# Two score banks of every third block move from ScalarE to VectorE as a bit-and-polynomial exponential

## The chip, the cores and the metric

The program runs on all 8 cores of one Trainium2 chip, each with its own 2048 tokens and no traffic between the cores. The metric is the device time in microseconds of the slowest core. Engines are named as in the profile: PE is TensorE, PEld its weight loads, DVE VectorE, ACT ScalarE, POOL GpSimd, SP SyncE. A matmul result lies in PSUM, which has 8 banks of 512 fp32 values in each of 128 partitions.

## The reference, cut to what matters

```python
x = x + attn(layernorm(x))           # first half
x = x + moe(layernorm(x))            # second half: top-1 router, 8 experts, relu
# attn, for each token and its 16 heads of 64 features:
Q = (X @ W_q + b_q) * scale; K = (X @ W_k + b_k) * scale; V = X @ W_v + b_v
Q, K, V = (t.reshape(n, heads, l, d) for t in (Q, K, V))
scores = jnp.einsum('neax,nebx->neab', Q, K)
A = jax.nn.softmax(scores, axis=2)
diag = jnp.diagonal(A, axis1=2, axis2=3)
out = (diag[..., None] * V).reshape(n, l, hid) @ W_o + b_o
```

The softmax runs along one axis and then only the diagonal is kept. So of every column of the score matrix only two numbers are needed: the exponential of its diagonal entry and the sum of the exponentials of all its entries. Because of the plain reshape, all 8192 entries of a column come from 512 neighbouring tokens and their 16 feature groups, so that a core works on four independent windows of 512 tokens.

## The kernel before, in words

**Windows, tiles, blocks.** NR = 4 windows w of 512 tokens, each of four tiles t of 128 tokens. A block r (0 to 63 in a window) is one tile with one feature group gb of its keys (r = 16 t + gb) against the 16 groups of queries: 16 matmuls of 64 rows by 512 columns, one PSUM bank each (line 443). A tile is 16 blocks.

**Slots.** ACT takes the exponential of 3 or 4 banks with one instruction, which also sums along the row (lines 563 and 567; the sum leaves ACT as a second instruction, ACTIVATION_READ_ACCUMULATOR). Such a group is a slot n. `SLOTS` gives the sizes of a block's five slots, (3,3,4,3,3) and (3,3,3,4,3) by turns; even slots use banks 0 to 3 and odd slots banks 4 to 6. PE may write slot n when ACT has done slot n-2 (`aE`), and ACT may read slot n when PE has written it (`pSCR`). A slot's sum is one column of ZC. The first `PLAIN` blocks of a window (18, 2, 2, 2) take the diagonal entry off before the exponential (line 563, as bias); the others need not when a bound on the scores, found on the chip for each window, is at most `LIMIT` (line 567).

**The fill.** All other work of PE goes through one bank, number 7 (`ONE_BANK`). It is a chain of generators, `fill`: the projections of the next window (query, key, value: 8 matmuls of 512 columns each), swaps and diagonals of the keys, and for each finished tile `tail`: the diagonal weights, the output projection, the residual, the router. After the matmuls of each slot PE takes units from this chain, by credits: a slot of 3 gives 1.5, a slot of 4 gives 2.5 (`SPARE`), a matmul of 512 columns costs 1. A yielded 0 ends the turn, and so does a yielded None (`breath`, at each job's start) if the turn has already done something. `hold` keeps the tail of tile t from beginning before block 16(t+1)+1 in the same window. At a window's end what is left of the chain is run without slots in between. PE calls `bank()` before each job and waits there for `vM`, until DVE has emptied bank 7 of the job before; everything PE does is in one order, so the next slot stands behind that wait.

**DVE** reads bank 7 job by job, in the same order (`bank()`, `query`, `key`, `value`, `swap_k`, `tail`). `PIECES` lists which jobs go into which tail. The key jobs are in the last two tiles of a window, for the window that follows. In `tail` DVE waits for the tile's last exponential (`aE`), sums ZC and goes on (lines 756 to 762, and on to 812, the last instruction of a tile's tail).

**Around it.** At the same time POOL issues the casting copies of the expert weights (w1b, w2b), one after the other. When the four windows are done the experts run. They are bound by PE; the change does not touch them.

Of the kernel before, what the change touches and what calls it, by code (L numbers as in the profile page):

```python
# [43 lines left out]

SLOTS = ((3, 3, 4, 3, 3), (3, 3, 3, 4, 3))
SPB = 5
SPH = 64 * SPB
SPT = 16 * SPB


# [16 lines left out]
LIMIT = 60.0  # L67
PLAIN = (18, 2, 2, 2)
ALL_BANKS = (7, 6, 5, 4, 3, 2, 1, 0)
# [3 lines left out]
def build_nc():  # L73
# [26 lines left out]
    with ExitStack() as st:  # L100
# [13 lines left out]
        XN2 = S("XN2", [P, 4, 1024], BF16)  # L114
# [44 lines left out]
        ZERO = S("ZERO", [P, 512], BF16)  # L159
# [48 lines left out]

        def piece_done(u):

            eg, i = divmod(u, NPC)
            return NCK * eg + (8 * i + 8 if i < 4 else NF + 2 * (i - 4) + 2)
# [14 lines left out]
        def _(e):  # L227
            ring, base, kM = ALL_BANKS, 0, 0

            def bank():  # L230
# [4 lines left out]
                kM += 1  # L235
                return ring[(kM - 1 - base) % len(ring)]

# [10 lines left out]
            def breath():  # L248

                yield None  # L250

# [48 lines left out]
            def bound(w):  # L300


                b = bank()
# [41 lines left out]
            def tail(w, t, pw, q):  # L345

                yield -(16 * q + 1)
# [47 lines left out]
                yield from pieces(pw, q, 2)  # L395
                b = bank()
# [10 lines left out]
                yield from pieces(pw, q, 3)  # L407
                b = bank()
# [12 lines left out]
            n = 0  # L421
            for w in range(NR):
# [6 lines left out]
                spare, hold = 0.0, 0  # L429
                for r in range(64):  # L430
                    t0, gb = divmod(r, NG)
# [5 lines left out]
                    for size in SLOTS[r % 2]:  # L437
                        if n >= 2:
                            e.wait_ge(aE, n - 1)
                        for i in range(size):  # L440
                            hp = (ga % 2) * 64
                            kb = KB if gb % 2 == ga % 2 else KS
                            mm = e.matmul(PS[:, (n % 2) * 4 + i, :],  # L443
                                          kb[w % 2][hp:hp + 64, gb // 2, t0 * P:(t0 + 1) * P],
                                          QB[w % 2][hp:hp + 64, ga // 2, :],
                                          start=True, stop=True, tile_position=(hp, 0))
                            ga += 1
                        mm.then_inc(pSCR, 1)
                        n += 1
                        spare = min(spare + SPARE[size], SPARE[size] + 1.0)  # L450
                        begun = False
                        while spare > 0 and r >= hold:
                            cost = next(fill, 0)
                            if cost is None:
                                if begun:
                                    break
                            elif cost < 0:
# [3 lines left out]
                            else:  # L461
                                spare -= cost
                                begun = True
                for _ in fill:
                    pass
# [85 lines left out]
        def _(e):  # L551
            for sb, srcap in first_loads:
                e.dma_start(out=sb[:], in_=srcap).then_inc(sINA, 16)
            def exps(w, r, less):

                t0, gb = divmod(r, NG)
                for i, size in enumerate(SLOTS[r % 2]):
                    n = SPH * w + SPB * r + i
# [72 lines left out]
        def _(e):  # L631
            ring, base, kM, nS = ALL_BANKS, 0, 0, 0

            def bank():

                nonlocal kM
                kM += 1
                e.wait_ge(pM, kM)
                return ring[(kM - 1 - base) % len(ring)]

            def step(op):

                nonlocal nS
                nS += 1
                op.then_inc(vS, 1)
                e.wait_ge(vS, nS)

            def moments(xt, mv):
                for i in range(2):
                    step(e.bn_stats(BN6[:, i, :], xt[:, i * 512:(i + 1) * 512]))  # L650
                step(e.bn_aggr(mv, BN6[:].rearrange("p a b -> p (a b)")))

            def stats():

                step(e.bn_aggr(MV[:], BNT[:].rearrange("p a b -> p (a b)")))
                step(e.tensor_scalar(NMN[:], MV[:, 0:1], -1.0, None, ALU.mult))
                step(e.tensor_scalar(NWH[:], MV[:, 1:2], 0.5, 0.5 * EPS, ALU.mult, ALU.add))
                step(e.tensor_scalar(NWI[:], NWH[:].bitcast(I32), 1, None, ALU.logical_shift_right))
                step(e.tensor_scalar(NWY[:].bitcast(I32), NWI[:], -1.0, MAGIC, ALU.mult, ALU.add))
                for _ in range(3):  # L660
                    step(e.scalar_tensor_tensor(NWU[:], NWY[:], NWY[:], NWH[:], ALU.mult, ALU.mult))
                    step(e.scalar_tensor_tensor(NWY[:], NWU[:], 1.5, NWY[:], ALU.subtract, ALU.mult))
# [5 lines left out]
            def tile_scales():  # L668

                step(e.tensor_scalar(NMX[:], MVX[:, :, 0], -1.0, None, ALU.mult))  # L670
                step(e.tensor_scalar(NXH[:], MVX[:, :, 1], 0.5, 0.5 * EPS, ALU.mult, ALU.add))
                step(e.tensor_scalar(NXI[:], NXH[:].bitcast(I32), 1, None, ALU.logical_shift_right))
                step(e.tensor_scalar(NWX[:].bitcast(I32), NXI[:], -1.0, MAGIC, ALU.mult, ALU.add))
                for _ in range(3):
                    step(e.tensor_tensor(NXU[:], NWX[:], NWX[:], ALU.mult))
                    step(e.tensor_tensor(NXU[:], NXU[:], NXH[:], ALU.mult))
                    step(e.scalar_tensor_tensor(NWX[:], NXU[:], 1.5, NWX[:], ALU.subtract, ALU.mult))

            def tile_norm(tc):
                e.tensor_scalar(XN[:, tc % 2, :], XA[:, tc, :], NMX[:, tc:tc + 1], NWX[:, tc:tc + 1],  # L680
                                ALU.add, ALU.mult).then_inc(vXN, 1)

# [5 lines left out]
            def query(w, mc):  # L688
# [5 lines left out]
                             apply_absolute_value=True)  # L694

            def swap_k(w, c):
# [10 lines left out]
                             apply_absolute_value=True)  # L707

            def bound(w):
                step(e.reduce_max(QM1[:], QMX[:, w % 2, :], axis=AX))  # L710
# [6 lines left out]
            def key(w, c):  # L717
                if c < DC:
# [5 lines left out]
                                    ALU.mult).then_inc(vPR, 1)  # L724
                if c > (1 if w == 0 else 0):
# [27 lines left out]
            def tail(w, t, pw, q):  # L753
                n = 4 * w + t
                e.wait_ge(sXR[t], 16 * (w + 1))
                step(e.tensor_tensor(XR[:, t, :], XR[:, t, :], BO[:], ALU.add))
                e.wait_ge(aE, SPH * w + SPT * (t + 1))
                step(e.reduce_sum(ZS[:], ZC[:, w % 2, NG * t:NG * (t + 1), :], axis=AX))  # L758
                step(e.reciprocal(ZS[:], ZS[:]))
# [10 lines left out]
                for hh in range(2):  # L770
# [4 lines left out]
                    step(e.bn_stats(BNT[:, hh, :], XR[:, t, hh * 512:(hh + 1) * 512]))  # L775
# [7 lines left out]
                step(e.scalar_tensor_tensor(LG[:], SWB[:], NMN[:], PS[:, b, 0:8], ALU.mult, ALU.add))  # L783
# [3 lines left out]
                step(e.reduce_max(RMX[:], LG[:], axis=AX))  # L787
                step(e.scalar_tensor_tensor(LW[:], LG[:], RMX[:], DESC[:], ALU.is_ge, ALU.mult))
                step(e.reduce_max(RM2[:], LW[:], axis=AX))
                e.tensor_scalar(MASK[:, n, :], LW[:], RM2[:], None, ALU.is_equal).then_inc(vMK, 1)  # L790
                e.wait_ge(vMK, n + 1)
                if w > 0:
                    e.wait_ge(sT2D[t], 16 * w)
                e.tensor_scalar(XN2[:, t, :], XR[:, t, :], NMN[:], NWY[:],
                                ALU.add, ALU.mult).then_inc(vXN2, 1)
                pieces(pw, q, 3)
# [364 lines left out]
```

## Time and profile before

| | us |
|---|---|
| median of 3 runs | 2745.1 |
| lowest and highest | 2744.68, 2861.35 |
| the profiled execution, its own time | 2744.31 |
| its span, slowest core (core 3) | 2742.7 |
| spans of the 8 cores | 2735.7 to 2742.7 |

The page of the profile gives for each engine its busy time, and that in 40 slices of the span. The attention part runs from the first exponentials at about 70 us to the last at 2097 us; the rest is the expert part. The time outside of the span is 1.6 us.

### The profile page before, as it was taken

Reading aid. Unit: us, or ns where it says so; the run is one execution under the profiler, and the core shown is the slowest. Engines: PE = TensorE matmul, PEld = TensorE weight load, DVE = VectorE, ACT = ScalarE, POOL = GpSimd, SP = SyncE. Lnnn points to the kernel's source line nnn. Section 1 sums busy time; section 2 is a strip of 40 time slices with the busy share of each in tenths; the row PEclk is TensorE's granted clock in tenths of the full one; section 3 lists DMA queues with packets and bytes.
Section 4 is the critical chain, followed back from the end, with each engine's and each line's share of the span. In section 5 each row is a group of like instructions: output and inputs, shape, how many; then the busy total and the mean of one; then the engine's idle time right before and its main releaser. Section 6 shows DMA issues by size and latency. Waiting matters only on the chain.

```text
span 2742.7 us, 31566 instructions; the slowest of 8 cores (2735.7 to 2742.7 us)
## 1 busy us (share of the span) xinstructions
PE 2190.7 (80%) x10600; PEld 829.8 (30%) x10600; DVE 580.7 (21%) x1309; ACT 2067.8 (75%) x2746; POOL 146.0 (5%) x201
## 2 busy tenths in 40 slices
PE   5877787877877787778687877767675999999997
PEld 2212121212111122111121212101111677777775
DVE  4322122212111222212122311101011122222221
ACT  2999999999999999999899999999995111111110
POOL 0000000000000000000100000000000011111100
PEclk9687676767677675856576777555555899999998
DMA  9999999999999999999600000120001577778762
GB/s 199 123 113 116 122 120 123 123 122 121 118 120 126 124 118 121 118 119 120 74 20 0 20 1 20 46 89 12 0 12 44 192 259 255 260 245 260 250 239 72
DMA packets 38165, 324.57 MB, mean 118 GB/s; under 512 B 8784, under 2 KB 9680, under 8 KB 25712
## 3 DMA queue, kind: packets, MB, share of 16 engines
q0 software_dynamic: 16224, 157.39, 48.5%
q1 hardware_dynamic: 21056, 164.98, 17.4%
q8 instruction: 95, 1.56, 0.2%
q14 instruction: 70, 0.57, 0.1%
q10 hardware_dynamic: 720, 0.08, 0.0%
HBM read 443.70 MB, written 159.73 MB: 220 GB/s over the span
## 4 chain that ended last, share of the span: by engine, by line
ACT 46%; PE 38%; issue 12%; DVE 1%; DMA 1%; POOL 0%; ACTq 0%; DVEq 0%; SPq 0%; POOLq 0%
ACT EA L567 22%; ACT EB L567 20%; PE PS L520 10%; PE PS L532 10%; PE PS L443 9%; PE PS L272 4%; ACT EA L563 2%; ACT EB L563 2%; PE PS L399 1%; PE PS L293 1%; PE PS L374 1%; PE PS L494 1%; DMA XA<-x 1%; PE PS L480 0%; PE PS L360 0%
## 5 line engine op out<-in xcount | busy, mean ns | idle before, releaser
L443 PE MATMUL PS<-AR 64*128 64x512 bf16 x4096 | 1089.2, 520 | 453.1 <-ACT EA L567 243.6
L567 ACT ACTIVATE EA<-PS 128x1536 bf16<-128x1536 f32 x580 | 958.1, 1652 | 29.4 <-PE PS L443 28.1
L567 ACT ACTIVATE EB<-PS 128x1536 bf16<-128x1536 f32 x580 | 858.9, 1481 | 27.4 <-PE PS L443 26.4
L443 PEld LDWEIGHTS PS<-AR 64*128 64x128 bf16 x4096 | 171.3, 99 | 1137.4 <-issue 1135.3
L272 PE MATMUL PS<-XLT,WR 128*128 128x512 bf16 x768 | 291.8, 468 | 6.8 <-DVE VB L732 2.3
L615 ACT ACTIVATE AR<-PS,B1C 128x320 bf16<-128x320 f32 x128 | 67.5, 527 | 226.4 <-PE PS L520 226.4
L532 PE MATMUL PS<-AR,WR 128*128 128x320 bf16 x1664 | 229.9, 299 | 0.0
L520 PE MATMUL PS<-AR,WR 128*128 128x320 bf16 x1600 | 224.2, 301 | 1.0 <-DVE AR L873 1.0
L621 ACT ACTIVATE XR<-PS,B2C 128x320 f32<-128x320 f32 x32 | 16.9, 527 | 270.7 <-PE PS L532 270.7
L532 PEld LDWEIGHTS PS<-AR,WR 128*128 128x128 bf16 x1664 | 162.1, 98 | 61.9
L520 PEld LDWEIGHTS PS<-AR,WR 128*128 128x128 bf16 x1600 | 157.4, 98 | 62.5 <-issue 1.3
L272 PEld LDWEIGHTS PS<-XLT,WR 128*128 128x128 bf16 x768 | 62.5, 105 | 261.9 <-issue 251.9
L567 ACT ACTIVATION_READ_ACCUMULATOR EB<-PS 128x1 f32 x580 | 137.7, 237 | 0.0
L567 ACT ACTIVATION_READ_ACCUMULATOR EA<-PS 128x1 f32 x580 | 136.6, 236 | 0.0
L898 DVE TENSOR_SCALAR AR<-PS,B1C 128x320 bf16<-128x320 f32 x128 | 70.3, 549 | 196.3 <-PE PS L520 176.6
L563 ACT ACTIVATE EA<-PS,NEGD 128x1536 bf16<-128x1536 f32 (+1 forms) x60 | 104.6, 1744 | 3.0 <-PE PS L443 3.0
L758 DVE TENSOR_REDUCE ZS<-ZC 128x16 f32<-128x80 f32 x16 | 3.8, 236 | 451.4 <-ACT EB L567 451.3
L563 ACT ACTIVATE EB<-PS,NEGD 128x1536 bf16<-128x1536 f32 x60 | 94.4, 1573 | 4.9 <-PE PS L443 4.6
L374 PE MATMUL PS<-WR,SA 128*128 128x512 bf16 x256 | 90.6, 436 | 1.5 <-DVE SA L766 1.1
L399 PEld LDWEIGHTS PS<-WRT,X1T 128*128 128x128 f32 x256 | 51.8, 281 | 50.3 <-issue 50.3
L1057 POOL DMA_DIRECT2D w1b<-w1t x64 | 31.6, 493 | 657.8 <-DMA w1b<-w1t 594.9
L720 DVE TENSOR_SCALAR AR<-PS,BKS 128x512 bf16<-128x512 f32 x32 | 24.0, 751 | 200.3 <-PE PS L272 200.3
(116 smaller groups left out, 1235.1 us busy)
## 6 DMA issues: line engine op xcount, KB each, us to landing
w1b<-w1t POOLq DMA_DIRECT2D x64, 1024.0 KB, 19.3
w2b<-w2t POOLq DMA_DIRECT2D x64, 1024.0 KB
WR<-w2b SPq DMA_DIRECT2D x26, 2048.0 KB
WR<-w1b SPq DMA_DIRECT2D x25, 2048.0 KB
XA<-w1b SPq DMA_DIRECT2D x7, 2048.0 KB
XA<-w2b SPq DMA_DIRECT2D x6, 2048.0 KB
XA<-x SPq DMA_DIRECT2D x16, 512.0 KB, 53.6
XR<-x SPq DMA_DIRECT2D x16, 512.0 KB, 44.4
```

Of the source, the lines that this page charges most:

```text
L272: mm = e.matmul(PS[:, b, :], WR[:, g, kc, mc * P:(mc + 1) * P], XLT[:, kc, :], start=(kc == 0), stop=(kc == DC - 1))
L293: mm = e.matmul(PS[:, b, 2 * t0:2 * t0 + 2], PROD[:, c % 2, t0 * P:(t0 + 1) * P], GM2[:], start=True, stop=True)
L374: mm = e.matmul(PS[:, b, :], SA[:, kc, :], WR[:, 3, kc, hh * 512:(hh + 1) * 512], start=(kc == 0), stop=(kc == DC - 1))
L399: mm = e.matmul(PS[:, b, 0:8], X1T[:, c, :], WRT[:, c, :], start=(c == 0), stop=(c == DC - 1))
L443: mm = e.matmul(PS[:, (n % 2) * 4 + i, :], kb[w % 2][hp:hp + 64, gb // 2, t0 * P:(t0 + 1) * P], QB[w % 2][hp:hp + 64, ga // 2, :], start=T ...
L520: mm = e.matmul(PS[:, b, 0:cols], w1[:, kc, (k % 8) * P:(k % 8 + 1) * P], XGF[:, eg % 2, kc, 0:cols], start=(kc == 0), stop=(kc == DC - 1))
L532: mm = e.matmul(PS[:, b, 0:cols], w2[:, j, (dc % 2) * P:(dc % 2 + 1) * P], HB[:, j, 0:cols], start=(j == 0), stop=(j == NF - 1))
L563: e.activation(EO[n % 2][:, 0:size * 512], scores, AF.Exp, bias=NEGD[:, w % 2, t0, gb:gb + 1], accum_out=ZC[:, w % 2, r, i:i + 1]).then_in ...
L567: e.activation(EO[n % 2][:, 0:size * 512], scores, AF.Exp, accum_out=ZC[:, w % 2, r, i:i + 1]).then_inc(aE, 1)
L615: e.activation(HB[:, k, 0:cols], PS[:, k % 4, 0:cols], AF.Relu, bias=B1C[:, ei * NF + k:ei * NF + k + 1]).then_inc(aCH, 1)
L898: e.tensor_scalar(HB[:, k, 0:cols], PS[:, k % 4, 0:cols], B1C[:, ei * NF + k:ei * NF + k + 1], 0.0, ALU.add, ALU.max).then_inc(vCH, 1)
L1057: e.dma_start(out=w1b[ei][i * 128:(i + 1) * 128, :], in_=w1t[ei][i * 128:(i + 1) * 128, :]).then_inc(sC1, 16)
```

## The change

In every third feature group (gb = 2, 5, 8, 11, 14: five blocks of each tile) a block that is not one of the first `PLAIN` is shared: ACT gets heads 0 to 13 in four slots, (4,3,4,3) or (3,4,3,4), and heads 14 and 15 go to DVE as one bank each, through bank 7. That is 15 blocks in the first window and 20 in each of the others, 75 blocks and 150 banks in all. A share may be made when at least `APART` = 4 slots have passed since the last one; PE does it in a `breath` of the fill, or directly after a slot when the fill is on hold or has ended, and it costs one credit. DVE subtracts the diagonal and clamps (one instruction from PSUM, which frees bank 7), and then seven passes over 128x512 fp32 values in SBUF make the exponential: the exponent from the bits, a polynomial for the mantissa, and a sum. The passes are placed between DVE's other jobs at build time by a clock that adds up assumed lengths; all that are left are run before the next share is taken.

```diff
-SLOTS = ((3, 3, 4, 3, 3), (3, 3, 3, 4, 3))
+def shared(w, r):
+    return r >= PLAIN[w] and r % NG % 3 == 2
...
+            if shared(w, r):
+                sizes = (4, 3, 4, 3) if n % 2 == 0 else (3, 4, 3, 4)
+            else:
+                sizes = (3, 3, 4, 3, 3) if n % 2 == 0 else (3, 3, 3, 4, 3)
...
+            def share():
+                nonlocal shared_at
+                shared_at = n
+                w, r, h = due.pop(0)
+                b = bank()
+                score(w, r, NG - 2 + h, PS[:, b, :]).then_inc(pM, 1)
+                SHARE[kM] = (w, r, h)
...
             def breath():
                 yield None
+                if due and n >= shared_at + APART:
+                    share()
+                    yield 1
+                    yield None
...
+                    if shared(w, r):
+                        due.append((w, r, 0))
+                    elif r > 0 and shared(w, r - 1):
+                        due.append((w, r - 1, 1))
...
+                        if due and (r < hold or not left) and n >= shared_at + APART:
+                            share()
+                            spare -= 1
...
+            def run_passes(until):
+                while clock <= until:
+                    if next(passes, None) is None:
+                        break
+            def take_share():
+                nonlocal passes
+                w, r, h = SHARE[kM + 1]
+                t0, gb = divmod(r, NG)
+                for _ in passes:
+                    pass
+                b = next_bank()
+                e.tensor_scalar(XP[:], PS[:, b, :], NEGD[:, w % 2, t0, gb:gb + 1], -CLAMP,
+                                ALU.add, ALU.max).then_inc(vM, 1)
+                e.wait_ge(vM, kM)
+                passes = exponential(w, r, h)
+            def exponential(w, r, h):
+                bits, ones = XP[:].bitcast(I32), MP[:].bitcast(I32)
+                step(PASS_LENGTH[0], e.tensor_scalar(bits, XP[:], CLAMP, LOG2E_23, ALU.min, ALU.mult))
+                step(PASS_LENGTH[1], e.tensor_scalar(ones, bits, MANTISSA, ONE, ALU.bitwise_and, ALU.bitwise_or))
+                step(PASS_LENGTH[2], e.tensor_scalar(bits, bits, EXPONENT, HALF_RANGE,
+                                     ALU.bitwise_and, ALU.bitwise_xor))
+                e.wait_ge(sZR, 32)
+                step(PASS_LENGTH[3], e.scalar_tensor_tensor(HP[:], MP[:], A3, MP[:], ALU.add, ALU.mult))
+                step(PASS_LENGTH[4], e.scalar_tensor_tensor(HP[:], HP[:], A2, MP[:], ALU.add, ALU.mult))
+                step(PASS_LENGTH[5], e.scalar_tensor_tensor(HP[:], HP[:], A1, MP[:], ALU.add, ALU.mult))
+                step(PASS_LENGTH[6], e.scalar_tensor_tensor(HP[:], HP[:], A0, XP[:], ALU.add, ALU.mult,
+                                            accum_out=ZD[:, w % 2, r // NG, r % NG // 3, h:h + 1]))
```

(The `yield True` after each pass is left out.) Beside this:

- `hold` lets a tail begin at block 16(t+1)+2, one block later, and then first makes the shares of its tile that are still due (`tile_shared`); each job of the fill, three more than before among them, starts with a `breath`.
- DVE's `tail` finishes the tile's passes, waits for `aE`, and adds ZD to ZC with two small instructions.
- XN2, the normalized rows on their way to memory, has two buffers instead of four, and its writer waits for the copy of two tiles before. The zeros that SP writes to xt2d lie in HP, and the first pass that writes HP waits for that copy (`sZR`).
- `LIMIT` is 40 instead of 60.
- After the last slot PE makes what shares are left before it goes to the last tail.

## Rows read from the trace of the kernel before

**Rows 1.** The page, parts 1 and 2: busy time, and tenths in 40 slices.
```profile
PE 2190.7 (80%) x10600; PEld 829.8 (30%) x10600; DVE 580.7 (21%) x1309; ACT 2067.8 (75%) x2746; POOL 146.0 (5%) x201
...
ACT  2999999999999999999899999999995111111110
...
PEclk9687676767677675856576777555555899999998
```
**Rows 2.** Windows of 100 us: length, busy PE, PEld, DVE, ACT, POOL, PEclk, DMA, GB/s.
```profile
455.00:555.00 100.00, 82.57 (x342) 24.99 (x339) 30.78 (x74) 93.94 (x122) 4.92 (x10) 0.74 1.01 123
...
1900.00:2000.00 100.00, 70.40 (x234) 11.09 (x234) 5.41 (x13) 99.25 (x132) 1.25 (x1) 0.54 0.00 0
...
2300.00:2400.00 100.00, 100.00 (x759) 73.48 (x758) 23.26 (x38) 15.29 (x29) 10.85 (x8) 1.00 0.80 260
```
**Rows 3.** Timeline (start, length in us, engine, line): slots with fill, full clock.
```profile
1105.10 1.47 ACT L567 ACTIVATE EA<-PS 128x1536 bf16<-128x1536 f32 x1
1105.37 0.59 PE L443 MATMUL PS<-AR 64*128 64x512 bf16 x3 [0.52 <-ACT EB L567]
1105.89 0.61 PE L272 MATMUL PS<-XLT,WR 128*128 128x512 bf16 x2
1106.53 1.48 ACT L567 ACTIVATE EB<-PS 128x1536 bf16<-128x1536 f32 x1
...
1110.80 1.93 ACT L567 ACTIVATE EA<-PS 128x2048 bf16<-128x2048 f32 x1
...
1112.65 1.51 ACT L567 ACTIVATE EB<-PS 128x1536 bf16<-128x1536 f32 x1
```
**Rows 4.** Timeline: slots without fill, half clock.
```profile
1942.61 1.01 PE L443 MATMUL PS<-AR 64*128 64x512 bf16 x3 [0.42 <-ACT EB L567]
...
1944.04 1.04 PE L443 MATMUL PS<-AR 64*128 64x512 bf16 x4 [0.42 <-ACT EA L567]
```
**Rows 5.** Windows of 5 us, columns as in rows 2: where ACT starves.
```profile
200.00:205.00 5.00, 1.82 (x12) 0.58 (x9) 2.76 (x6) 3.11 (x5) 0.49 (x1) 0.91 1.06 118
...
975.00:980.00 5.00, 4.91 (x14) 0.81 (x15) 0.69 (x1) 4.06 (x6) 0.49 (x1) 0.50 0.96 106
...
2015.00:2020.00 5.00, 4.45 (x17) 1.80 (x16) 0.96 (x5) 4.63 (x7) 0.00 (x0) 0.50 0.00 0
```
**Rows 6.** DVE's groups by line and shape: busy us, mean ns of one, idle before.
```profile
L720 DVE TENSOR_SCALAR AR<-PS,BKS 128x512 bf16<-128x512 f32 x32 | 24.0, 751 | 200.3 <-PE PS L272 200.3
L772 DVE TENSOR_TENSOR XR<-PS,XR 128x512 f32<-128x512 f32 x32 | 22.1, 692 | 186.4 <-PE PS L374 186.4
...
L698 DVE CAST AR<-PS 128x512 bf16<-128x512 f32 x32 | 22.1, 690 | 0.7
L703 DVE TENSOR_REDUCE KMX<-AR 128x1 f32<-128x512 bf16 x32 | 21.6, 675 | 0.0
L756 DVE TENSOR_TENSOR XR<-XR,BO 128x1024 f32<-128x1024 f32 x16 | 19.6, 1224 | 0.0
L680 DVE TENSOR_SCALAR XN<-XA,NMX,NWX 128x1024 bf16<-128x1024 f32 x16 | 12.8, 805 | 0.1
```
**Rows 7.** Timeline of DVE: two small steps in a row, each waiting for the last.
```profile
1061.84 0.15 DVE L809 CAST SLI<-SLF 128x1 int32<-128x1 f32 x1
1062.10 0.15 DVE L810 TENSOR_SCALAR SLA<-SLI 128x1 int32<-128x1 int32 x1
```
**Rows 8.** Timeline of DVE: two key jobs; a tail's last instruction; the tile's end.
```profile
474.51 0.75 DVE L720 TENSOR_SCALAR AR<-PS,BKS 128x512 bf16<-128x512 f32 x1 [6.75 <-PE PS L272]
...
484.68 0.75 DVE L720 TENSOR_SCALAR AR<-PS,BKS 128x512 bf16<-128x512 f32 x1 [5.26 <-PE PS L272]
...
554.68 0.16 DVE L812 SCALAR_TENSOR_TENSOR SLT<-SLA,SLB 128x1 int32<-128x1 int32 x1
...
573.73 0.23 DVE L758 TENSOR_REDUCE ZS<-ZC 128x16 f32<-128x80 f32 x1 [17.72 <-ACT EB L567]
```
**Rows 9.** Waits of PE: engine line <- releaser: us in total, times, longest.
```profile
PE PS L272 <- DVE VB L732: 2.3, 8, 0.4
```

More of the change, by code:

```diff
@@ L300, in bound @@
             def bound(w):
+                yield from breath()
                 b = bank()
@@ L440, in _ @@
                         for i in range(size):
[L441 to L446, printed above, removed]
+                            mm = score(w, r, ga, PS[:, (n % 2) * 4 + i, :])
                             ga += 1
@@ L450, in _ @@
                         spare = min(spare + SPARE[size], SPARE[size] + 1.0)
+                        if due and (r < hold or not left) and n >= shared_at + APART:
+                            share()
+                            spare -= 1
                         begun = False
-                        while spare > 0 and r >= hold:
-                            cost = next(fill, 0)
+                        while spare > 0 and r >= hold and left:
+                            cost = next(fill, -64)
                             if cost is None:
@@ L632, in _, with made_at, spend @@
             ring, base, kM, nS = ALL_BANKS, 0, 0, 0
-            def bank():
-                nonlocal kM
+            clock, passes = 0.0, iter(())
+            SLOT_AT = [0.0]
+            for w, r in BLOCKS:
+                for size in BLOCKS[w, r][1]:
+                    SLOT_AT.append(SLOT_AT[-1] + SLOT_LENGTH[size])
+            def made_at(k):
+                return SLOT_AT[max(MADE[k] - 1, 0)]
+            def spend(length):
+                nonlocal clock
+                clock += length
@@ L644, in step @@
+            def step(length, op):
+                nonlocal nS, clock
                 nS += 1
+                clock += length
                 op.then_inc(vS, 1)
@@ L753, in tail @@
             def tail(w, t, pw, q):
+                nonlocal clock
                 n = 4 * w + t
                 e.wait_ge(sXR[t], 16 * (w + 1))
[L756 to L759, printed above, removed]
+                step(1.3, e.tensor_tensor(XR[:, t, :], XR[:, t, :], BO[:], ALU.add))
+                first = [r for r in range(NG * t, NG * t + NG) if shared(w, r)]
+                while kM + 1 in SHARE and SHARE[kM + 1][0] == w and SHARE[kM + 1][1] in first:
+                    take_share()
+                for _ in passes:
+                    pass
+                clock = max(clock, SLOT_AT[tile_end(w, t)])
+                e.wait_ge(aE, tile_end(w, t))
+                if first:
+                    a, b = first[0], first[-1] + 1
+                    step(0.27, e.tensor_tensor(ZDT[:], ZD[:, w % 2, t, :, 0], ZD[:, w % 2, t, :, 1],
+                                               ALU.add))
+                    step(0.27, e.scalar_tensor_tensor(
+                        ZC[:, w % 2, a:b:3, SPB - 1], ZDT[:], 0.5 * POLY,
+                        NUM[:, w % 2, :, :].rearrange("p t g -> p (t g)")[:, a:b:3],
+                        ALU.mult, ALU.mult))
+                step(0.27, e.reduce_sum(ZS[:], ZC[:, w % 2, NG * t:NG * (t + 1), :], axis=AX))
+                step(0.27, e.reciprocal(ZS[:], ZS[:]))
                 e.tensor_tensor(DGT[:], ZS[:], NUM[:, w % 2, t, :], ALU.mult).then_inc(vDG, 1)
```

183 lines of the change are left out of this document (123 added, 60 removed).

## The prediction, as it was put before the kernel ran

> **What bounds the kernel now.** I read the page's busy times first, then windows of 100 us, then the timeline of single slots, and last windows of 5 us. The page shows two parts [rows 1]: ACT nine tenths busy or more in nearly every slice to about slice 30, then PE. In two windows of the first part, one in a tile of key jobs and one with hardly any fill, ACT is busy 93.9 and 99.3 us of 100 while DVE has 31 and 5; in the second PE is at 100 [rows 2]. So ACT's exponentials set the pace up to 2097 us, and only what shortens them there shortens the kernel.
>
> The timeline gives a slot's real length, start to start, since the read of the sum overlaps the next exponential: 1106.53 - 1105.10 = 1.43 us for three banks and 1112.65 - 1110.80 = 1.85 us for four [rows 3]. A block before is 4 x 1.43 + 1.85 = 7.57 us, a tile 16 x 7.57 = 121 us.
>
> PE is the near second, and its clock decides how near. At the full level a slot's matmuls take 0.59 us and two fill matmuls 0.61, and PE then waits 0.52 us for ACT [rows 3]. At the half level (1.2 GHz) the matmuls take 1.01 us, and without fill PE still waits 0.42 us [rows 4]; with fill it does not fit, and ACT starves: at 975 us the granted clock is 0.50, PE has 4.91 of 5 us and ACT 4.06 [rows 5]. Of the 378 windows of 5 us from 200 to 2090 us, 91 have ACT under 4.85 us; rows 5 hold the first, one from the middle and the last. That is 24% of the time, in which PE sets the pace.
>
> **The change, part by part.**
>
> ACT: a shared block has two slots of four and two of three, 2 x 1.85 + 2 x 1.43 = 6.56 us, 1.01 less. For 75 blocks this is **-75.8 us**. It is the most that the change can bring directly.
>
> PE: it does the same 16 matmuls of a block. Three banks cost it as much as four (1.01 and 1.04 us [rows 4]), since neighbouring heads sit in different halves of the array. Before, a block is five slots; after, four slots and two lone matmuls, about 4 x 1.01 + 2 x 0.49 = 5.0 us at half clock against 5.05: nothing. In the 24% where PE sets the pace, a faster ACT brings nothing: 0.24 x 75.8 = 18 us would be lost. But a shared block also offers fewer credits to the fill (8.0, of which 2 go to shares, against 8.5), so part of the fill moves to the idle end of the tile. I take half, **+9 us** (bounds 0 and 18).
>
> DVE, per share: the read of bank 7 is like line 720, 0.75 us. Three passes have one SBUF source. Line 680 does 1024 values in 0.805 us, where line 756 with two sources needs 1.224 [rows 6], so 512 values cost about 0.45 (upper bound 0.69). Four passes have two fp32 sources like lines 756 and 772, 0.69 each. Reading out the sum has no row on DVE; I put it at 0.2, a little over the small steps of rows 7 (0.15). Small steps that wait for each other start 0.26 us apart for 0.15 of work [rows 7], so each of eight steps adds 0.1. Sum: 0.75 + 1.35 + 2.76 + 0.2 + 0.8 = 5.9 us. A tile with ten shares adds 59 us to what DVE has now, 31% at most [rows 2] or some 36 us a tile, about 95 of 118 us. DVE fits on average, on work that is hidden under ACT. What isn't hidden is lateness: PE's next job, and behind it the next slot, waits for bank 7.
>
> A single late pass (at most 0.8 us) is mostly covered: a job's last matmul ends a turn, the next slot's matmuls follow (0.6 or 1.0 us), and ACT has a slot in hand. PE's waits of this kind are tiny now: the projections waited 2.3 us in all for DVE, 8 times [rows 9]. The two shares of a block lie about one block apart, 6.6 us, then there is a gap of two. In the 6.6 us DVE must end the passes of the first before it frees the bank of the second. With queries or values around it 5.9 + 1.2 = 7.1 us is 0.5 late, which is covered. With keys it is not: a key job is 0.75 + 0.69 + 0.69 + 0.17 + 2 x 0.68 = 3.7 us, with gaps 4.1 (the product and the diagonal among them, taken as 0.69 and 0.17 like their neighbours), every 10.2 us [rows 6 to 8], so 5.9 + 2.7 = 8.6 us is 2.0 late, some 1.0 of it beyond what a turn and ACT's slot in hand cover. About 21 of the 75 pairs lie among keys (the last tile and a part of the third in three windows): **+20 us**. Bounds: 0, and 120 if each of 150 shares costs a whole pass of 0.8.
>
> The fill's end: in a window's last tile it now ends 573.7 - 554.7 = 19 us early [rows 8], 2.5 blocks or 21 credits. The change takes 8.5 (one block later), 2.5 (the shared blocks) and 10 (shares), 21, and breaths split turns further. So the fill just misses the window's end, and a few jobs with their DVE answers run with no slot beside them. For three windows **+8 us** (bounds 0 and 30). In the other tiles the overrun falls into the two blocks in which the next tail is on hold.
>
> The end: the last share's 5.9 us of passes start near the last slots and two small steps are added before the last tail, whose chain is exposed: **+3 us** (0 to 7).
>
> At nothing: the first HP write waits for a copy issued some 100 us before; XN2's writer waits for a copy of two tiles (250 us) before. No DMA is added. POOL's casting copies have ended long before 1900 us (0 GB/s there [rows 2]), and their readers come after that, so some slowing there is covered. The new LIMIT changes nothing: from the inputs the bound is about 2.
>
> Sum, on the profiled execution's 2744.3 (0.8 under the median): 2744.3 - 75.8 + 9 + 20 + 8 + 3 = 2708.5, in the median's terms **2709 us**, 1.3% less.
>
> **A rule against it.** Rows 6 show no large SCALAR_TENSOR_TENSOR; the nearest rows, TENSOR_TENSOR with two fp32 sources, run at (1.224 - 0.692)/512 = 1.04 ns a value. The Trainium skill, "Vector Engine (DVE) Microarchitecture Reference", section "Points that are easy to get wrong", says that this form of instruction (S2S2D2_STT) with two SBUF sources that are not bf16 halves its throughput; no run shown here tests it. By it the result would be the third rival below.
>
> **The rivals.**
>
> 1. *Nearly all of the gain is realized*: DVE is never late by more than is covered, and the thinner fill lets ACT starve less. For it: 76% of the time PE has 0.4 to 0.5 us a slot to spare. Against it: DVE at 80% with hand-placed passes. 2744.3 - 75.8 + 3 (end) = 2672; with the fill's end, 2680.
>
> 2. *Slower: bank 7 is held at every share.* PE issues in one order; if DVE still has a pass before it takes the share, the slot behind waits. Without stalls the gain is 75.8 - 20 = 56, so 0.37 us of ACT's time lost per share (150) leaves nothing, and 0.74 makes it 2% slower. With 0.8, a whole pass, it is 2744.3 - 56 + 120 = 2808. For it: at the half clock nothing covers a delay, and that is where PE is full [rows 5]. Against it: the two shares have 6.6 us or more for 5.9 of work, and PE's present waits on DVE are tiny [rows 9].
>
> 3. *The passes with two fp32 sources run at half rate.* From rows 6, 0.53 us more for each of four, a share of 8.0 us: a tile needs 80 + 36 = 116 of 118 us of DVE, and the second share of each pair is 8.0 + 1.2 - 6.6 = 2.6 late, over 1 us uncovered, times 75, plus 40 for the keys: 2744.3 - 56 + 115 = 2803. For it: only the rule named above. Against it: the rows of the two-source kind at full rate.
>
> That the change doesn't do what it says is not likely: the shared blocks all lie where line 567 runs.
>
> **How the numbers follow.** My forecast (stalls mostly among keys, 2690 to 2735): 0.50, own range 2690 to 2735. Rival 1 (2665 to 2690): 0.27. A milder form of rival 2, 0.2 to 0.7 us lost per share, 2735 to 2800: 0.15. Rival 2 in full and rival 3, over 2800: 0.04 and 0.04. The range for 8 in 10 goes into rival 1's and to the beginning of the milder rival 2's: 2672 to 2752. Two per cent, about what a measurement of this kernel can tell from no change, is 55 us: faster than 2690 has 0.27, slower than 2800 has 0.08, the rest 0.65.
>
> **What would show it.** In the profile after: slots of line 567 at unchanged lengths, 1205 instead of 1280; span from first to last exponential shorter by 35 us or so. DVE busy 21% up to about 50%; the two-source passes at 0.69 us (right) or 1.2 (rival 3); read of a share at 0.75. PE's waits on DVE for bank 7 a few tens of us, mostly in the last tile of a window; if they sum to over 60 us and are spread over all tiles, rival 2. ACT's idle time by tile: unchanged in tiles of values and queries, larger with keys. The forecast is wrong if a share's DVE work is far from 5.9 us, if the clock's share of half level changes much (PE a little denser or thinner), or if the fill falls behind by more than two blocks in ordinary tiles.

## The result and the profile after

The changed kernel takes 3009.1 us (median of 4 runs), against 2745.7 for the kernel before beside it: a ratio of 1.095, with a 95% interval of 1.0935 to 1.0965. It is 9.5% slower, where 1.3% faster was forecast, and far outside of the range. (A few runs of any kernel fall into a slower state of the chip; the ratios leave them out and the medians don't, so the two can stand a little apart.)

The page of the changed kernel, parts 1 and 2, beside [rows 1]:

```profile
span 3004.0 us, 34251 instructions; the slowest of 8 cores (2991.7 to 3004.0 us)
## 1 busy us (share of the span) xinstructions
PE 2241.5 (75%) x10523; PEld 859.8 (29%) x10600; DVE 1294.9 (43%) x2689; ACT 2009.4 (67%) x2596; POOL 148.2 (5%) x201
...
ACT  2998887777788777777888777889998411111110
...
PEclk8886676656566666575667665755555599999999
```

ACT has less to do, and yet from the fourth slice on, the first with shared blocks throughout, it is mostly busy seven to eight tenths instead of nine. DVE is at 43%, so it is not full. Three engines wait for each other, and none is the bound by its work. The groups of the exponentials (busy us, mean ns of one, idle before) give the size:

```profile
L658 ACT ACTIVATE EA<-PS 128x2048 bf16<-128x2048 f32 x307 | 580.0, 1889 | 81.5 <-PE PS L291 81.0
L658 ACT ACTIVATE EB<-PS 128x1536 bf16<-128x1536 f32 x542 | 791.9, 1461 | 192.5 <-PE PS L291 189.9
L658 ACT ACTIVATE EA<-PS 128x1536 bf16<-128x1536 f32 x236 | 344.8, 1461 | 84.5 <-PE PS L291 83.9
```

In the whole attention part from 200 us on, ACT's idle time before its exponentials, added up row by row from the timeline, was 57 us before and is 376 us now: +319. Its busy time fell by 2067.8 - 2009.4 = 58. The difference, +261, is that of the spans (3004.0 - 2742.7 = 261). So the saving is there, less some 18 us, and five times as much is lost in waiting for PE. Most of the 18 us comes with the waits: 229 slots instead of 95 are followed by one of over 0.15 us, and then a slot of three takes ACT 1.54 us instead of 1.42, as the read of its sum has no next exponential to run under (134 x 0.12 = 16 us).

What PE waits for, in the view of its waits (engine line <- releaser: us in total, times, longest). Before, the projections' wait for DVE was 2.3 us in all [rows 9]; now:

```profile
PE PS L352 <- DVE XP L766: 87.5, 28, 6.6
PE PS L364 <- DVE XP L766: 60.3, 18, 4.9
PE PS L457 <- DVE XP L766: 38.0, 13, 4.5
PE PS L483 <- DVE XP L766: 36.3, 9, 5.3
```

Line 766 is DVE's read of a share out of bank 7. With four smaller lines PE waits 262 us for it, 89 times, 2.9 us on average and 6.6 at most. That isn't one pass in flight (0.8 us), that is several. The waits lie in every tile that has shares, 4 to 26 us in each.

The timeline of one case tells why (start, length, engine, line, and in brackets the idle time before). Line 352 are the matmuls of a projection, line 843 is DVE's read of a query, lines 774 to 788 are the passes:

```profile
892.11 0.75 DVE L766 TENSOR_SCALAR XP<-PS,NEGD 128x512 f32<-128x512 f32 x1 [0.18 <-DVE HP L788]
892.96 0.43 DVE L774 TENSOR_SCALAR XP<-XP 128x512 int32<-128x512 f32 x1
893.49 1.06 PE L352 MATMUL PS<-XLT,WR 128*128 128x512 bf16 x2 [2.03 <-ACT EB L658]
893.50 0.43 DVE L776 TENSOR_SCALAR MP<-XP 128x512 int32<-128x512 int32 x1
...
898.71 0.39 PE L352 MATMUL PS<-XLT,WR 128*128 128x512 bf16 x1
...
899.21 0.75 DVE L843 TENSOR_SCALAR AR<-PS,BQS 128x512 bf16<-128x512 f32 x1 [5.29 <-PE PS L352]
...
900.11 0.37 PE L291 MATMUL PS<-AR 64*128 64x512 bf16 x1 [0.29 <-DVE AR L843]
...
900.68 0.42 DVE L778 TENSOR_SCALAR XP<-XP 128x512 int32<-128x512 int32 x1
901.27 0.69 DVE L782 SCALAR_TENSOR_TENSOR HP<-MP 128x512 f32<-128x512 f32 x1 [0.18 <-DVE XP L778]
902.07 0.69 DVE L784 SCALAR_TENSOR_TENSOR HP<-HP,MP 128x512 f32<-128x512 f32 x1
902.86 0.69 DVE L786 SCALAR_TENSOR_TENSOR HP<-HP,MP 128x512 f32<-128x512 f32 x1
903.66 0.69 DVE L788 SCALAR_TENSOR_TENSOR HP<-HP,XP 128x512 f32<-128x512 f32 x1
...
904.53 0.75 DVE L766 TENSOR_SCALAR XP<-PS,NEGD 128x512 f32<-128x512 f32 x1 [0.18 <-DVE HP L788]
...
905.54 1.01 PE L352 MATMUL PS<-XLT,WR 128*128 128x512 bf16 x2 [4.29 <-DVE XP L766]
...
907.61 1.45 ACT L658 ACTIVATE EB<-PS 128x1536 bf16<-128x1536 f32 x1 [4.23 <-PE PS L291]
```

DVE takes a share at 892.11 and does two of its seven passes. Then its queue says: wait for the next query, whose first matmul has begun at 893.49 and whose last ends at 899.10. DVE stands idle for 5.29 us, with five passes to do that wait for nothing. The next share's matmul runs at 900.11 and has ended by 900.5, but the five passes come first, since the read of a share overwrites XP, which they still use; it is read at 904.53. PE is held for 4.29 us, and ACT idles for 4.23. DVE is idle and late at the same time.

Over the timeline of the attention part from 200 us on, DVE is idle for 891 us in gaps over 0.3 us. In 876 of them it waits for PE, and in 647 of these (174 gaps) passes of the last share are still to be done.

The code has the reason, in lines that the shortened diff ahead doesn't show. The build-time clock asks when a job of bank 7 will be there, and takes the number of slots at which PE claimed the bank:

```python
            def bank():                       # TensorE
                if kM - base >= len(ring):
                    e.wait_ge(vM, kM - len(ring) + 1)
                kM += 1
                MADE[kM] = n                  # slots issued when the job BEGINS
                ...
            def made_at(k):                   # VectorE
                return SLOT_AT[max(MADE[k] - 1, 0)]
```

A projection has eight matmuls spread over four or five turns, 5.6 us in the case above. DVE's `bank()` calls `run_passes(made_at(kM + 1))`, which fills DVE's queue up to the first of them and puts the wait there, but the wait ends with the last.

### The profile page after: what moved, and what is told of

Same layout as the page of the kernel before. It is cut to its first block, busy times and chain, and to the rows that moved or that the text cites. A ratio compares the mean times of both kernels' runs of the same rounds, so it can differ in the third digit from the quotient of the medians.

```text
span 3004.0 us, 34251 instructions; the slowest of 8 cores (2991.7 to 3004.0 us)
## 1 busy us (share of the span) xinstructions
PE 2241.5 (75%) x10523; PEld 859.8 (29%) x10600; DVE 1294.9 (43%) x2689; ACT 2009.4 (67%) x2596; POOL 148.2 (5%) x201
## 4 chain that ended last, share of the span: by engine, by line
PE 45%; ACT 24%; DVE 19%; issue 11%; DMA 1%; DVEq 1%; POOL 0%; another core or an unknown queue 0%; ACTq 0%; SPq 0%; POOLq 0%
PE PS L291 12%; ACT EA L658 10%; PE PS L611 9%; PE PS L623 9%; ACT EB L658 9%; PE PS L352 7%; DVE XP L766 2%; PE PS L457 2%; DVE HP L788 2%; ACT EA L654 2%; DVE HP L786 2%; DVE HP L784 2%; ACT EB L654 2%; DVE HP L782 2%; PE PS L373 2%
## 5 line engine op out<-in xcount | busy, mean ns | idle before, releaser
L291 PE MATMUL PS<-AR 64*128 64x512 bf16 x4096 | 1105.8, 537 | 359.0 <-ACT EA L658 179.7
L658 ACT ACTIVATE EA<-PS 128x2048 bf16<-128x2048 f32 (+1 forms) x543 | 924.7, 1703 | 166.0 <-PE PS L291 164.9
L658 ACT ACTIVATE EB<-PS 128x1536 bf16<-128x1536 f32 x542 | 791.9, 1461 | 192.5 <-PE PS L291 189.9
L766 DVE TENSOR_SCALAR XP<-PS,NEGD 128x512 f32<-128x512 f32 x150 | 112.7, 751 | 115.1 <-PE PS L291 95.4
L457 PE MATMUL PS<-WR,SA 128*128 128x512 bf16 x240 | 105.6, 525 | 48.9 <-DVE XP L766 38.0
L658 ACT ACTIVATION_READ_ACCUMULATOR EB<-PS 128x1 f32 x542 | 116.7, 215 | 0.0
L658 ACT ACTIVATION_READ_ACCUMULATOR EA<-PS 128x1 f32 x543 | 116.5, 215 | 0.0
L782 DVE SCALAR_TENSOR_TENSOR HP<-MP 128x512 f32<-128x512 f32 x150 | 103.7, 691 | 23.8 <-DVE XP L778 23.4
L786 DVE SCALAR_TENSOR_TENSOR HP<-HP,MP 128x512 f32<-128x512 f32 x150 | 103.8, 692 | 15.6
L788 DVE SCALAR_TENSOR_TENSOR HP<-HP,XP 128x512 f32<-128x512 f32 x150 | 103.7, 691 | 15.0 <-DVE HP L786 0.5
L784 DVE SCALAR_TENSOR_TENSOR HP<-HP,MP 128x512 f32<-128x512 f32 x150 | 103.6, 691 | 13.3
```

Source lines behind the costliest of these rows:

```text
L291: return e.matmul(out, kb[w % 2][hp:hp + 64, gb // 2, t0 * P:(t0 + 1) * P], QB[w % 2][hp:hp + 64, ga // 2, :], start=True, stop=True, tile ...
L457: mm = e.matmul(PS[:, b, :], SA[:, kc, :], WR[:, 3, kc, hh * 512:(hh + 1) * 512], start=(kc == 0), stop=(kc == DC - 1))
L658: e.activation(EO[n % 2][:, 0:size * 512], scores, AF.Exp, accum_out=ZC[:, w % 2, r, i:i + 1]).then_inc(aE, 1)
L766: e.tensor_scalar(XP[:], PS[:, b, :], NEGD[:, w % 2, t0, gb:gb + 1], -CLAMP, ALU.add, ALU.max).then_inc(vM, 1)
L782: step(PASS_LENGTH[3], e.scalar_tensor_tensor(HP[:], MP[:], A3, MP[:], ALU.add, ALU.mult))
L784: step(PASS_LENGTH[4], e.scalar_tensor_tensor(HP[:], HP[:], A2, MP[:], ALU.add, ALU.mult))
```

## The experiments

The theory, P: the passes stand in DVE's queue behind waits for jobs that PE has only begun; the remainder is flushed in front of the next share, and holds PE and ACT. The rivals: C, DVE has too much to do between two shares, however they stand (the reason given in the prediction for tiles of keys); B, one bank for fill and shares holds PE up whatever DVE does.

**The slot number of the last matmul.** In the eight jobs of more than one turn:

```diff
-                mm.then_inc(pM, 1)
+                made(mm)              # mm.then_inc(pM, 1); MADE[kM] = n
```

> The changed kernel with one difference: the slot number that the build-time clock of VectorE takes for a job of bank 7 is that of the job's last matmul, not that of its first. The work and TensorE's order stay the same; only VectorE's passes move ahead of its waits. Theory P (placement: the passes stand in VectorE's queue behind a wait for a job that TensorE has only begun, and a share then waits for them): 2680 to 2760 us, TensorE's waits on the read of a share under 60 us instead of 262. Rival C (capacity: VectorE has too much work between two shares wherever the passes stand): over 2900 us, the waits nearly as long. Rival B (the ring: one bank shared by fill and shares holds TensorE up whatever VectorE does): over 2900 us.

2743.1 us, ratio 0.997 (0.994 to 0.999) to the kernel before: 266 us less than the changed kernel, for the same instructions of PE and DVE in another order on DVE alone. The waits of PE for the read of a share:

```profile
PE PS L488 <- DVE XP L771: 16.8, 8, 3.3
PE PS L357 <- DVE XP L771: 12.3, 16, 1.7
PE PS L378 <- DVE XP L771: 7.0, 3, 2.4
PE PS L462 <- DVE XP L771: 5.2, 6, 1.3
```

In all they are 44 us (39 waits) instead of 262, ACT's idle time is 124 us instead of 376, and DVE's idle time with passes left 98 us instead of 647 (summed in the same way). P holds: the order of DVE's passes explains the whole loss against the kernel before. C and B fall as its explanation. The 266 us are not PE's waits alone. These fell by 219 us, and PE's own busy time fell too, for the same matmuls, as its granted clock rose (windows of the attention part from 200 us on: length, busy PE, PEld, DVE, ACT, POOL, PEclk, DMA, GB/s; the changed kernel, then this run):

```profile
200.00:2358.00 2158.00, 1502.00 (x5407) 374.45 (x5471) 1079.78 (x2292) 1779.74 (x2257) 74.37 (x129) 0.62 0.55 71
...
200.00:2092.00 1892.00, 1440.39 (x5470) 363.51 (x5470) 1081.09 (x2292) 1766.49 (x2256) 74.48 (x130) 0.67 0.63 81
```

The kernel before has 0.67 as well, so with the stalls PE runs more of its time at the half level, and 62 us more of busy time go with it. DVE's busy time is the same in both rows, 1080 and 1081 us.

**Half of the dose.** The number half-way between a job's first and last matmul:

```diff
-                MADE[kM] = n
+                MADE[kM] = (MADE[kM] + n) // 2
```

> The kernel of e1_made_at_end with the slot number half-way between a job's first and last matmul. Theory P: VectorE's passes are placed for half of the time that it waits, so some are left in front of the shares: between 2743 and 3009 us, 2790 to 2900 us, with TensorE's waits on the read of a share between 45 and 262 us. If something else in that edit made the difference, it is near one of the ends.

2867.2 us, 1.044 (1.042 to 1.046), near the middle of 2743 and 3009 (2876), and PE's waits for the shares' reads are 155 us, the middle of 44 and 262 being 153. So the lateness grows with the error of the recorded slot; DVE's idle time with passes left is 448 us, between 98 and 647.

**Shares further apart.** In the changed kernel, `APART = 6` instead of 4.

> The changed kernel with APART 6 instead of 4, nothing else: two shares are at least six slots (9 us) apart, which is more than the 5.9 us that one takes on VectorE and a query or value beside it. If shares are late because the second of a pair comes too soon (the reason given in the prediction for tiles of keys), TensorE's waits on the read of a share fall from 262 to under 80 us and the time to under 2850 us. Theory P (the passes stand behind waits for jobs that have only begun, whatever the distance): over 2950 us, waits over 200 us.

2978.0 us, 1.083 (1.074 to 1.091), the waits 216 us, and DVE still idles 563 us with passes left. The distance between shares, which the prediction took as the cause of lateness, is worth 31 us of 266 here.

**All passes at once.** Behind the read of a share its seven passes run without a break:

```diff
-                passes = exponential(w, r, h)
+                for _ in exponential(w, r, h):
+                    pass
```

> The changed kernel with the seven passes run at once after the read of a share, so that none is ever left in front of the next share; other jobs of bank 7 can wait up to 5.2 us for them instead. Theory P: the waits of TensorE for the read of a share are gone, those on other reads grow to at most 150 times 2 us; 2720 to 2880 us. Rival C: 2950 us or more, as the work is the same.

2922.8 us, 1.058 (1.041 to 1.075), slower than I expected by theory P (2720 to 2880). The shares are read in time (33 us of waits), but now the other jobs of bank 7 stand behind up to 5.2 us of passes:

```profile
PE PS L373 <- DVE AR L852: 90.7, 23, 4.9
PE PS L443 <- DVE SA L939: 42.6, 12, 4.3
PE PS L472 <- DVE X1T L951: 36.1, 12, 3.9
```

I had reckoned with 2 us a share at most; the short jobs (swap of the keys, output weights) follow each other from turn to turn, and one late read there holds PE for 4 us. DVE's busy time is nearly that of the run of 2743 us (1306 and 1297 us), so the order alone is worth 180 us here.

**No passes, and no shares.** The first reads the 150 banks and leaves out the seven passes, so the sums lack two heads of each shared block; the second leaves the two heads out altogether, passes and all. (Both set ZD to zero once, at the start.)

```diff
-                passes = exponential(w, r, h)
```

> The changed kernel without the seven passes: VectorE reads each of the 150 shares out of bank 7 and does no more with them, so the sums of the softmax lack these two heads. Theory P and rival C: 2675 to 2710 us, since ScalarE has 76 us less to do and nothing is in front of a read. Rival B: over 2850 us.

```diff
-                    if shared(w, r):
-                        due.append((w, r, 0))
-                    elif r > 0 and shared(w, r - 1):
-                        due.append((w, r - 1, 1))
```

> The changed kernel without the shares: the two heads of the 75 blocks are left out altogether, TensorE doesn't make them and VectorE doesn't read them. It is the floor of what ScalarE's shorter blocks can bring. All theories: 2665 to 2695 us. The distance to the run without passes is the price of 150 lone matmuls and reads through bank 7: under 15 us by theory P and rival C, most of the 260 us by rival B.

2714.4 us, 0.981 (0.965 to 0.997), and 2660.0 us, 0.963 (0.954 to 0.971). The floor is 85 us under the kernel before, and 82 by the spans of the profiles (2661.1 and 2742.7). ACT's time outside of these idle times, from 200 us to the last exponential, fell by 80 us (1838.8 to 1759.0), 4 more than the 75.8 of the prediction; its idle time hardly changed (57 and 55). From there a share with nothing behind it costs 54 us, well placed passes 29 more (2743.1 - 2714.4). The first term was put at +9 for PE's bound and +8 for the fill's end.

**What the 54 us are.** The turns cut and charged as if there were shares, but neither matmul nor read:

```diff
-                b = bank()
-                score(w, r, NG - 2 + h, PS[:, b, :]).then_inc(pM, 1)
-                SHARE[kM] = (w, r, h)
```

> The changed kernel with neither the passes nor the lone matmuls nor their reads; the two heads are left out, but TensorE's turns are cut and charged as if the shares were made (a credit and an ended turn for each). Between the kernel without shares (2660 us) and the one without passes (2714 us): if the 54 us come from the cut turns and the credits, which make the fill end later, 2700 us or more; if they come from the matmuls and the reads of bank 7, 2660 to 2675 us.

2693.3 us, 0.980 (0.978 to 0.982): by the times, 33 of the 54 us are the broken turns of the fill, 21 the matmuls and reads. The ratios alone would not part this run from the one without passes (0.981, 0.965 to 0.997), but the profiled spans do: 2661.1, 2691.7 and 2714.0 us. The expectation allowed for one or the other; it is both.

A part of the 33 has a place. At the start of each later window ACT now waits for the leftovers of the fill:

```profile
1061.58 1.54 ACT L651 ACTIVATE EB<-PS,NEGD 128x1536 bf16<-128x1536 f32 x1 [4.11 <-PE PS L291]
```

These three gaps are 12.5 us in all, and none of them is there in the kernel before or in the one without shares. In the run of 2743 us they are 19.7.

**Placed behind a slot of three.** Three banks cost PE as much as four (1.01 and 1.04 us [rows 4]), and neighbouring heads lie in different halves of the array. From this I argued that a lone matmul behind a slot of three might cost nothing. Of the shares, 96 instead of 50 stand behind such a slot with a head of the other half.

> The kernel without the seven passes (e2_no_passes, 2714 us, 54 us over the one without shares) with the shares paired as in h2_paired, so that VectorE's passes have no part in it. If the 54 us are lone matmuls in a full TensorE, 46 more in pairs take 10 to 17 us of them: 2700 us. If they are the wait for the bank, 2712 us or more.

Ratio 0.991 (0.987 to 0.996), median 2741.4 us: not better than the 0.981 (0.965 to 0.997) unpaired. Having both shares of a block due at once moved some in front of the short statistics chain (the waits there rose from 12.3 to 24.3 us), so this run doesn't tell what pairing itself is worth.

**Towards a kernel that gains.** From the run of 2743 us on, first: DVE takes a share that is due before that statistics chain, instead of behind it.

```diff
                 pieces(pw, q, 2)
+                while kM + 1 in SHARE:
+                    take_share()
                 stats()
```

> The kernel with the slot number of the last matmul, and one more difference: in each tail VectorE reads a share that is due before the short chain of statistics instead of behind it (8 waits of 2.8 to 3.3 us stand there now, 17 us in all). If such waits reach ScalarE in full: 12 to 17 us less than that kernel, 2728 us; if the window's end and the half clock take most of what is left, 5 us or less.

2724.8 us, 0.991 (0.988 to 0.995): 18 us less by the medians, 15 by the ratios. The eight waits there (16.8 us) are gone; those elsewhere grew by 9, so that PE's waits for shares are 36 us instead of 44. ACT's idle time fell by 17 us, from 124 to 107. Then the leftovers of the fill at a window's end:

```diff
-                fill = chain(first, *[tail(w, t, w, t + 1) for t in range(3)])
+                fill = chain(fill, first, *[tail(w, t, w, t + 1) for t in range(3)])
...
-                for _ in fill:
-                    shared_at = -APART
```

(The loop over what is left now stands behind the last window only.)

> The kernel of b_share_before_stats, and what is left of the fill at the end of a window is not run there without slots but carried into the next window's first turns. ScalarE stood idle 6.4 to 6.8 us at each of three window ends there. If nothing takes its place, 15 to 19 us less than that kernel: 2708 us, about 0.985 of the kernel before. If the work only moves into turns that are full, 0.99.

2716.8 us, 0.987 (0.983 to 0.991). Before it, ACT's row at a window's end read

```profile
1077.57 1.54 ACT L659 ACTIVATE EB<-PS,NEGD 128x1536 bf16<-128x1536 f32 x1 [6.41 <-PE PS L296]
```

and now

```profile
1074.86 1.54 ACT L660 ACTIVATE EB<-PS,NEGD 128x1536 bf16<-128x1536 f32 x1 [3.48 <-PE PS L296]
```

The three gaps went from 19.6 to 10.7 us. This is the best version found, 1.3% under the kernel before, with the same work as the changed one. A second XP, so that a share can be read while passes of the last are left, was not tried.

What did not help: fewer shares in full tiles and more in the last three, more in the last three alone, pairing, the tail one block earlier, and other credits.

> As the last, with the shares where there is room: three blocks of each full tile instead of five, and seven of each of the last three tiles, in which the fill is short; 114 banks instead of 150. ScalarE's saving is 57 blocks times 1.01 = 58 us. If what a share costs in a full tile is TensorE's and VectorE's overload, it falls faster than their number: 2700 us. If each share has a fixed price of about 0.4 us or more wherever it stands: 2725 us or more.

2739.2 us, 0.996 (0.993 to 0.999): 114 banks do less well than 150, though ACT's gaps at the window ends are gone (0 instead of 19.6 us). So in full tiles a well placed share seems to earn something still; the last three tiles differ too.

> As b_share_before_stats, with seven blocks instead of five shared in each of the last three tiles and five in the others; 162 banks. Against that kernel it tells what two more shared blocks bring in a tile with a short fill: 6 us in all if they are free there. Against c_fewer_shares it tells what the last two shared blocks of a full tile bring: 20 us or more less if there is still room, more time if the tile is full.

No ratio could be formed; in the profiles it is within the cores' spread of b_share_before_stats (2711.6 to 2727.0 us and 2713.0 to 2721.1). Nothing is shown.

> As h1_carry_over, and a share is made behind a slot of three whose last matmul is in the other half of the array where that is possible: 96 of 150 shares instead of 50, with both shares of a block due at once. If a lone matmul costs TensorE its own 0.2 to 0.5 us and one in a pair nothing, as slots of three and four cost it the same, the 46 bring 8 to 15 us where TensorE is the bound: 2697 us, 0.981. If the price of a share lies in the wait for bank 7 and not in the matmul, nothing.

2724.2 us, 0.990 (0.985 to 0.994), against 0.987 (0.983 to 0.991) unpaired: no gain that can be told.

> As h2_paired, with the tail beginning one block earlier, as in the kernel before (block 16(t+1)+1). If the fill's late end matters, 5 to 10 us less than h2_paired; if the tail then waits for VectorE's last passes of the tile, 10 us more or worse.

2743.5 us, 0.997 (0.995 to 0.999): worse than h2_paired. The wait for the tile's passes outweighs the earlier start, as the second case of the expectation has it: PE waits for DVE's DGT at the start of a tail 23 us, 11 times, against 5.1 us, 3 times, in h2_paired.

> The kernel of h1_carry_over, and a share made inside of the fill ends the turn but is charged no credit. The run with the turns alone says that cut and charged turns cost 33 us of 54. If it is the credits (the fill ends later and runs beside more slots than it needs), 2690 to 2705 us. If it is the ended turn itself, no change from 2717 us. If TensorE is simply full there, more time.

No ratio could be formed; the profiled run took 2727.0 us, against 2717: no gain.

> As y1_no_credit with slightly larger credits for every slot (1.6 and 2.8 instead of 1.5 and 2.5). If the fill ends too late in full tiles, 5 to 15 us less than y1_no_credit; if turns then hold up ScalarE at the half clock, 10 us more or worse.

2773.7 us, 1.011 (1.009 to 1.012). The gaps at the window ends are gone, but ACT's idle time is 153 us instead of y1_no_credit's 110, and PE waits 77 us for shares instead of 40. So of the 33 us of broken turns it is not the credit that costs, as far as these two runs tell. 12.5 of them are the late end of the fill; how the broken turn costs the other 20 stays open.

## Why the prediction was wrong, point by point

- **ACT's saving**, -75.8 us: right in size. The slots keep their lengths (start to start, where ACT does not wait, 1.42 and 1.87 us at the median in both kernels) and 1205 are left; without shares the kernel is 85 us faster.
- **DVE's work per share**, 5.9 us: right. The groups of the changed kernel:

```profile
L766 DVE TENSOR_SCALAR XP<-PS,NEGD 128x512 f32<-128x512 f32 x150 | 112.7, 751 | 115.1 <-PE PS L291 95.4 <-DVE HP L788 19.7
L786 DVE SCALAR_TENSOR_TENSOR HP<-HP,MP 128x512 f32<-128x512 f32 x150 | 103.8, 692 | 15.6
...
L776 DVE TENSOR_SCALAR MP<-XP 128x512 int32<-128x512 int32 x150 | 64.0, 427 | 16.2 <-DVE XP L774 1.4
...
L788 DVE DVE_READ_ACCUMULATOR HP<-HP,XP 128x1 f32 x150 | 12.3, 82 | 0.0
```

  The parts of a whole share are 0.75 + 3 x 0.43 + 4 x 0.69 + 0.08 = 4.9 us of work; with the gaps it takes 5.6 us where nothing comes between, in the run with all passes at once. (The prediction set them against 118 us a tile; by its own slots a tile with five shared blocks is 16 x 7.57 - 5 x 1.01 = 116 us, which changes nothing in its argument.)
- **DVE's lateness**, +20 us with an upper bound of 120: this is the step that failed. It said that what isn't hidden is lateness, and then sized it by the distance between the two shares of a block, as if DVE ran a pass whenever it had nothing else. DVE runs what its queue says next. What had to be asked was where in the queue each pass stands, in front of or behind which wait, and what that wait ends with. That was in the full diff, as the slot number taken in `bank()`, and I read past it. The runs show about 266 us for it: 2743 with the number mended, 3009 as it was. Nor does it lie among the keys: the last tiles of the three windows, where the prediction had most of it, have 57 of the 262 us of waits. Well placed, the passes cost 29 us (2743 against 2714), near the +20; whether they do so for the prediction's reason, two shares of a block too close, no run tells.
- **The bound.** A whole pass of 0.8 us for each share is no upper bound when all seven can stand in front of one. From the prediction's own terms, the last five passes are 0.45 + 4 x 0.69 + 5 x 0.1 = 3.7 us with gaps (3.7 in the example too), and 150 times that is some 555 us; an upper bound so far out would have held the result. Rival 2 had the right place (bank 7, PE's one order) and the wrong price; it was given 0.04, its milder form 0.15.
- **PE's share of the work at nothing, fill +9 and +8:** too low. Shares without passes cost 54 us, of which 33 are broken turns. Counting PE's matmuls per block did not show them. The fill's late end was foreseen in kind and is larger than +8: 12.5 us of ACT's idle time with the turns alone, 19.7 in the run of 2743 us.
- **The end, +3:** about right. From the last exponential to the end of the span it is 645.2 us before, 645.7 in the changed kernel and 648.5 in the run of 2743 us.
- **The account.** With each term from a run, 2745 - 85 (ACT) + 54 (shares without passes) + 29 (passes, well placed) + 266 (their place in the queue) = 3009 us. These are differences of neighbouring runs, so that they add up is no test; the sizes are what the prediction has to be held against.
- **Rival 3** (half rate of the passes with two fp32 sources): wrong. Lines 782 to 788 take 691 to 692 ns, the same as a TENSOR_TENSOR of that size [rows 6]. The sentence of the Trainium skill on it ("Vector Engine (DVE) Microarchitecture Reference", section "Points that are easy to get wrong") doesn't hold for this instruction here.
- **What would show it**: the prediction named the sign (waits for bank 7 over 60 us and spread over all tiles mean rival 2), and that is what the profile after has.

## What to carry to other kernels

When work is placed by hand into an engine's gaps, the gap is not the engine's idle time but the stretch in front of a particular wait in its queue; find out for each wait when it ends, not when what it waits for begins. An engine that is 43% busy can be late for 2.9 us on average, 89 times. An upper bound for lateness is all the work that the queue can hold in front of the urgent instruction, not the length of one piece. And in a trace, idle time of an engine that has work left which depends on nothing is the first thing to look for: here it was 647 of 891 us. An engine's stalls can also lower the clock that the engine it holds up is granted, 0.67 to 0.62 for PE here.

## What the runs showed of the hardware

- SCALAR_TENSOR_TENSOR with immediate scalars, two fp32 sources in SBUF, 128x512: 691 to 692 ns, no slower than the TENSOR_TENSOR of line 772 (692 ns, one source in PSUM), and 82 ns more for the read of its sum (0.2 us had been assumed).
- TENSOR_SCALAR on int32 with bit operations, 128x512 in SBUF: 422 to 427 ns, against 751 for an fp32 source in PSUM (line 766). They run at the rate that line 680 showed for fp32, 805 ns for 1024 values [rows 6].
- PE's granted clock in the attention part is 0.67 before, 0.62 in the changed kernel and 0.67 again with DVE's passes in better places and PE's instructions the same; at 0.62 PE's busy time is 62 us more.
